# Edge counts from one moving operand, and a new spread of scatters and gathers over the phases

## The reference, cut to what matters

```python
z = jax.ops.segment_sum(ex, dst, num_segments=n)          # attention: sums over the edges of a node
seg = edge_type * n + dst
agg = jax.ops.segment_sum(x[src], seg, num_segments=N_REL * n)
cnt = jax.ops.segment_sum(ones, seg, num_segments=N_REL * n)
mean = agg.reshape(N_REL, n, -1) / jnp.maximum(cnt, 1.0).reshape(N_REL, n, 1)
h1 = jnp.einsum('rni,rio->no', mean, W_rel) + x @ W_root + b_rgcn
deg = jax.ops.segment_sum(ones, dst, num_segments=n) + 1.0
```

## Time and profile before

| | us |
|---|---|
| median of 3 runs (lowest, highest) | 1623.46 (1621.61, 1624.95) |
| the profiled execution's own time | 1636.26 |
| its span | 1634.5 |
| edge, from 0 to | 177.7 |
| g1 to | 237.2 |
| a1 to | 426.8 |
| g2 to | 479.4 |
| a2 to | 542.2 |

### The profile page before, as it was taken

The page is one execution under the profiler, slowest core; times in us unless marked ns, Lnnn a source line. Parts: engine busy times, 40 slices in busy tenths (PEclk is TensorE's granted clock), DMA queues, the critical chain, the costliest instruction groups (busy, mean ns, idle before and its releaser), DMA issues. The chain is left out here.

```text
span 1634.5 us, 30722 instructions
## 1 busy us (share of the span) xinstructions
PE 1325.3 (81%) x9518; PEld 971.8 (59%) x9519; DVE 913.9 (56%) x1669; ACT 650.1 (40%) x954; POOL 607.3 (37%) x737
## 2 busy tenths in 40 slices
PE   8998485781377669987799999999999938749888
PEld 6766464781264446765666666666666626445566
DVE  8941667793254544225556665566666537656710
ACT  8964410881312334004255555455555433022300
POOL 0086555776556100001355555555555510000000
PEclk9999595795587679996899999999999968958989
DMA  1000200000200411008599999899999868233300
GB/s 57 1 1 1 80 16 1 1 1 0 77 10 1 117 58 58 1 19 298 182 260 287 260 277 290 231 291 288 281 279 276 243 177 233 60 119 116 115 20 29
DMA packets 103603, 208.90 MB, mean 128 GB/s; under 512 B 23346, under 2 KB 48399, under 8 KB 103420
## 3 DMA queue, kind: packets, MB, share of 16 engines
q1 hardware_dynamic: 75484, 145.72, 26.1%
q0 software_dynamic: 28064, 62.47, 16.7%
HBM read 195.14 MB, written 36.43 MB: 142 GB/s over the span
## 5 line engine op out<-in xcount | busy, mean ns | idle before, releaser
L641 PE MATMUL r_pO<-ring,r_rowsT 128*128 x2520 | 421.0, 326 | 0.0
L641 PEld LDWEIGHTS r_pO<-ring,r_rowsT 128*128 128x128 f16 x2520 | 243.8, 98 | 153.9
L1695 DVE SCALAR_TENSOR_TENSOR ring<-q_wstage,ring 128x768 f16<-128x768 f32 x198 | 175.2, 953 | 55.6 <-ACT ring L1654 50.2
L1635 POOL DMA_INDIRECT acc_dram<-r_msg,r_scol x70 | 127.9, 1826 | 158.7 <-PE r_pT L1755 98.9
L1654 ACT ACTIVATE ring<-q_wstage 128x768 f16<-128x768 f32 x198 | 148.8, 829 | 26.4 <-issue 26.4
L474 POOL DMA_INDIRECT inv_col<-qinv_dram,pair_col x112 | 119.8, 1070 | 78.9 <-POOL pair_col L487 71.3
L387 PE MATMUL acc<-oh_d,oh_s 125*125 125x512 f16 (+1 forms) x800 | 143.4, 310 | 4.5 <-issue 3.2
L424 POOL DMA_INDIRECT slot_dram<-table_record,table_rowi x80 | 101.7, 1271 | 103.9 <-issue 103.2
L1683 ACT ACTIVATE r_msg<-r_pO,slot_inv 128x768 f32<-128x768 f32 x70 | 62.8, 897 | 192.1 <-PE r_pO L641 159.8
L1702 DVE TENSOR_TENSOR r_rowsT<-r_pT,r_rowsT 128x512 f16<-128x512 f32 x71 | 48.8, 687 | 106.9 <-ACT r_rowsT L1663 97.6
L1755 PE MATMUL r_pT<-r_S,q_parts 128*128 128x128 f16 x852 | 102.0, 223 | 7.6 <-issue 6.8
(11 more groups left out here) (363 smaller groups left out, 2494.1 us busy)
## 6 DMA issues: line engine op xcount, KB each, us to landing
q_wstage<-in_L_gnn_W_rel_dram SPq DMA_DIRECT2D x33, 2304.0 KB
f_stage<-in_L_ffn_w_dram SPq DMA_DIRECT2D x12, 768.0 KB, 4.5
stage<-in_L_gnn_W_dram SPq DMA_DIRECT2D x6, 768.0 KB, 5.7
q_wstage<-in_L_ffn_w_fast_dram SPq DMA_DIRECT2D x6, 768.0 KB, 5.0
q_wstage<-in_L_ffn_w_slow_dram SPq DMA_DIRECT2D x6, 768.0 KB, 7.0
q_wstage<-in_L_ffn_h_fast_dram SPq DMA_DIRECT2D x6, 768.0 KB, 8.7
f_stage<-in_L_ffn_w_fast_dram SPq DMA_DIRECT2D x6, 768.0 KB, 4.4
f_stage<-in_L_ffn_w_slow_dram SPq DMA_DIRECT2D x6, 768.0 KB, 6.0
```

What stands on the lines that cost most here:

```text
L641: ins = eng.matmul(out, x, w[:, h * n:(h + 1) * n], start=first and x is xh and w is wh, stop=last and x is xl, **kw)
L1635: eng.indirect_dma_start(out=K.acc_dram[u % 2], out_offset=bass.IndirectOffsetOnAxis(ap=scol[:, u:u + 1], axis=0), in_=msg[:, u, :], in_of ...
L1695: ins_ = eng.scalar_tensor_tensor(wring[:, slot, 1, k, :], wstage[:, slot, k, :], W_SCALE, wring[:, slot, 0, k, :], ALU.mult, ALU.subtract)
```

## The change

The relation one-hot of a column is no longer a strided view of `R`: VectorE writes it (34 wide) behind the source one-hot in the same place of the ring, which grows to 659 columns. The products are taken the other way round: the destination one-hot is the stationary operand for all, and source and relation are moved through together. A row tile takes two matmuls, of 512 and of 147 columns. The sums stand transposed in PSUM, so that the copies come out as `CT` at once, and `K.counts` is what the transposes give; the mask and the degrees hang on the copies and no longer on the transposes. The scatters run in three blocks, 40 in edge, 28 in g1 and 12 at the start of a1, and the load of the slot table moves behind the last of them, to a1. The gathers are spread as 56 in a1, 20 in g2 and 36 in a2.

```diff
--- before.py
+++ after.py
-TABLED_FIRST = 46
-INV_A1, INV_G2 = 68, 88
+TABLED_EDGES, TABLED_G1 = 40, 68
+INV_A1, INV_G2 = 56, 76
...
-        oh_s = sb("oh_s", [EP, HOTS, N], FP16)
+        oh_s = sb("oh_s", [EP, HOTS, N + REL], FP16)
...
+            TAIL = REST + REL
+
+            def tail_at(i):
+                return 5 + i // 3, i % 3 * TAIL
 
             def count_piece(i, piece):
                 if piece == 0:
                     return acc[0:P, i, :], slice(0, 512)
-                b, o = (5, i * REST) if i < 4 else (6, 0)
-                return acc[0:P, b, o:o + REST], slice(512, N)
+                b, o = tail_at(i)
+                return acc[0:P, b, o:o + TAIL], slice(512, N + REL)
...
-                scatter_records(K, eng, s["tabled"], 0, TABLED_FIRST)
-                eng.wait_ge(s["tabled"], 16 * TABLED_FIRST)
+                scatter_records(K, eng, s["tabled"], 0, TABLED_EDGES)
+                eng.wait_ge(s["tabled"], 16 * TABLED_EDGES)
...
                         eng.wait_ge(s["hots_free"], j + 1)
-                        eng.tensor_scalar(oh_s[:, u, :], iota_n[:, :], srcf[:, j:j + 1], None, ALU.is_equal).then_inc(s["hots_s_ready"], 1)
+                        eng.tensor_scalar(oh_s[:, u, N:], iota_g[0:EP, :], etf[:, j:j + 1], None, ALU.is_equal)
+                        eng.tensor_scalar(oh_s[:, u, 0:N], iota_n[:, :], srcf[:, j:j + 1], None, ALU.is_equal).then_inc(s["hots_s_ready"], 1)
...
                 eng.wait_ge(s["products_done"], 1)
-                a, cols = count_piece(NT - 1, 1)
-                eng.tensor_copy(K.counts[:, NT - 1, cols], a).then_inc(s["rest_stored"], 1)
-                link(eng.tensor_scalar(qinv[:, :, :], acc[0:P, 6, REST:REST + NT * REL].rearrange("p (i r) -> p i r", r=REL), 1.0, W_SCALE,
-                                       ALU.max, ALU.mult))
+                for b, i0, n in ((5, 0, 3), (6, 3, 2)):
+                    tails = acc[0:P, b, 0:n * TAIL].rearrange("p (i r) -> p i r", r=TAIL)
+                    eng.tensor_copy(CT[0:P, i0:i0 + n, 512:N], tails[:, :, 0:REST]).then_inc(s["rest_stored"], 1)
+                    last = eng.tensor_scalar(qinv[:, i0:i0 + n, :], tails[:, :, REST:TAIL], 1.0, W_SCALE, ALU.max, ALU.mult)
+                link(last)
...
                 for i in range(NT):
-                    for piece in range(2 if i < NT - 1 else 1):
-                        a, cols = count_piece(i, piece)
-                        eng.copy(K.counts[:, i, cols], a).then_inc(s["counts_stored"], 1)
+                    eng.copy(CT[:, i, 0:512], acc[0:P, i, :]).then_inc(s["ct_stored"], 1)
...
                     for t in range(NT):
-                        tile = slice(t * P, (t + 1) * P)
-                        at = REST + t * REL
-                        eng.matmul(acc[0:P, 6, at:at + REL], oh_d[:, u, tile], onehot, start=False, stop=False, **kw)
                         for piece in range(2):
                             a, cols = count_piece(t, piece)
-                            last = eng.matmul(a, oh_s[:, u, tile], oh_d[:, u, cols], start=False, stop=False, **kw)
+                            last = eng.matmul(a, oh_d[:, u, t * P:(t + 1) * P], oh_s[:, u, cols], start=False, stop=False, **kw)
...
@@ gat_project, sync @@
-            if heads > 1:
-                eng.wait_ge(s["tabled"], 16 * (EJ - TABLED_FIRST))
-                eng.dma_start(K.table["tables"][:, :, :, :].rearrange("t a l b -> t a (l b)"),
-                              K.slot_dram.rearrange("(a t l) b -> t a (l b)", a=2, l=128)).then_inc(K.s_table_loaded, 16)
@@ gat_project, gpsimd @@
-                scatter_records(K, eng, s["tabled"], TABLED_FIRST, EJ)
+                scatter_records(K, eng, K.s_tabled, TABLED_EDGES, TABLED_G1)
@@ gat_attend, sync @@
+            if heads > 1:
+                eng.wait_ge(K.s_tabled, 16 * (EJ - TABLED_EDGES))
+                eng.dma_start(K.table["tables"][:, :, :, :].rearrange("t a l b -> t a (l b)"),
+                              K.slot_dram.rearrange("(a t l) b -> t a (l b)", a=2, l=128)).then_inc(s["table_loaded"], 16)
@@ gat_attend, gpsimd @@
                 eng.sem_inc(s["out_free"], 2)
+                scatter_records(K, eng, K.s_tabled, TABLED_G1, EJ)
                 eng.wait_ge(s["columns_ready"], 1)
                 gather_inverse_counts(K, eng, s, 0, INV_A1)
```

More of the change, by code:

```diff
@@ L355, in _ @@
                 for i in range(NT):
-                    for piece in range(2 if i < NT - 1 else 1):
-                        a, cols = count_piece(i, piece)
-                        eng.copy(K.counts[:, i, cols], a).then_inc(s["counts_stored"], 1)
+                    eng.copy(CT[:, i, 0:512], acc[0:P, i, :]).then_inc(s["ct_stored"], 1)
                 for i in range(NT):
                     eng.wait_ge(s["transposed"], i + 1)
-                    eng.copy(CT[:, i, :], acc[0:P, 2 * (i % 2):2 + 2 * (i % 2), :].rearrange("p b n -> p (b n)")[:, 0:N]).then_inc(s["ct_stored"], 1)
+                    eng.copy(K.counts[:, i, :], acc[0:P, 2 * (i % 2):2 + 2 * (i % 2), :].rearrange("p b n -> p (b n)")[:, 0:N]).then_inc(s["counts_stored"], 1)
             @block.tensor
@@ L401, in _ @@
                 zeros((6,), P, False, True).then_inc(s["products_done"], 1)
-                eng.wait_ge(s["counts_stored"], 2 * NT - 1)
-                eng.wait_ge(s["rest_stored"], 1)
+                eng.wait_ge(s["ct_stored"], NT)
+                eng.wait_ge(s["rest_stored"], 2)
                 for i in range(NT):
                     if i >= 2:
-                        eng.wait_ge(s["ct_stored"], i - 1)
+                        eng.wait_ge(s["counts_stored"], i - 1)
                     for k in range(NT):
@@ L410, in _ @@
                         lo, hi = k * P, (k + 1) * P
-                        src = K.counts[:, k, i * P:(i + 1) * P]
+                        src = CT[:, k, i * P:(i + 1) * P]
                         if hi <= 512:
@@ L675, in gat_project @@
         W = Weights(K, name + "_w", rows_view(w), B["stage"], B["wparts"])
-        s = {n: K.sem(name + "_" + n) for n in ("a_loaded", "projected", "h_ready", "ones_ready", "pair_ready", "tabled"
+        s = {n: K.sem(name + "_" + n) for n in ("a_loaded", "projected", "h_ready", "ones_ready", "pair_ready"
                                                 ) + tuple("gathered_%d" % b for b in range(IDX_BUFS))}
@@ L764, in gat_attend @@
         s = {n: K.sem(name + "_" + n) for n in ("cs_ready", "als_ready", "max_done", "uv_made", "uv_ready", "bc_ready", "rows_copied", "t1_ready", "arg_ready",
-                                                "e_ready", "p_ready", "pv_done", "out_free", "finish_a", "finish_b", "bias_loaded", "pair_ready", "table_turned", "columns_ready"
+                                                "e_ready", "p_ready", "pv_done", "out_free", "finish_a", "finish_b", "bias_loaded", "pair_ready", "table_loaded", "table_turned", "columns_ready"
                                                 ) + tuple("gathered_%d" % b for b in range(IDX_BUFS))}
@@ L935, in spread_sources @@
                 spread(2 * b, B["cur"][:, b, 0, :]).then_inc(s["als_ready"], 1)
-            turns(eng, spread_sources, between=lambda: turn_tables(K, eng, K.s_table_loaded, psum[:, 6, 0:4 * T1]).then_inc(s["table_turned"], 1))
+            turns(eng, spread_sources, between=lambda: turn_tables(K, eng, s["table_loaded"], psum[:, 6, 0:4 * T1]).then_inc(s["table_turned"], 1))
             def multiply(h, b):
@@ L991, in gat_phase @@
             B["stage"][0:P, :, :].rearrange("p k n -> p (k n)"), B["parts"][:, :, :, :].bitcast(FP32).rearrange("p i a c -> p (i a c)"))]
-        K.s_table_loaded = K.sem("table_loaded")
+        K.s_tabled = K.sem("slots_tabled")
         gat_project(K, "g1", B, B["g"], norm, ins["L0_gnn_W1"], ins["L0_gnn_a_src1"], ins["L0_gnn_a_dst1"], HEADS, HD, h1)
```

5 lines of the change are left out of this document (1 added, 4 removed).

## The result

Twelve runs of each kernel: 1620.54 us median before (1618.25 to 1625.19), 1625.68 after (1623.28 to 1628.76). The ratio after to before is 1.0028, with a 95% interval of 1.0017 to 1.0038: 0.28% or 4.5 us slower (the medians lie 5.1 apart), where 2.4 us faster was forecast. The time lies in the range given, on the other side of no change.

A forecast was written before the change was run, and what follows sets the result against it. TensorE was taken to bound edge and GpSimd a1, with a2 close; edge would become GpSimd's. Edge -10.3, a1 -12.1 and a2 +20.0 made -2.4 us from 1623.46: 1621.1, range 1604 to 1629 (the forecast's own 1615 to 1626).

The forecast's parts named there:

- TensorE's column: Edge phase: a row tile falls from 0.338 to 0.280 us, a column from 1.69 to 1.40.
- rival 3: Edge: TensorE's column does not shrink, phase ends at 159 to 161, total 1629.4 us, slower; chance 0.12.
- The 34-wide one-hots: Edge, VectorE: each added instruction costs 0.09 us, 4 us over 46 columns less 0.9 of waits, ranks 3.2 later.
- The products' end: Edge: VectorE as the late feeder takes TensorE's one-hot products to 132 us.
- The 40 scatters: Edge, GpSimd: first starts at 85.2, all 40 take 64.7 us (bounds 59.4 and 68), ending at 149.9.
- The row shows none of it: Edge: no sign of VectorE's one-hots locking GpSimd's ports; if so, scatters would be held up to 13 us.
- The end of edge: GpSimd takes the bound from TensorE; with landing 1.45 and barrier 0.8 the phase ends at 152.2 us.
- The slow stretch: Edge, 104 to 144 us: TensorE's slowdown, worth 15.2 us, belongs to the profiled execution alone.
- rivals 1 and 2: Edge: slow stretch in every run; 1: goes with the change, 1605.9 us, chance 0.22; 2: stays, 1614.7, chance 0.10.
- a1 and a2: a1: late table +12.2, twelve gathers fewer -24.3, so -12.1 us; a2: twelve more, 24.3 less 4.25 cover, +20.0.
- g1 and g2: 28 scatters in g1 and 20 gathers in g2 bound neither phase: no change.
- the edge term: Edge phase in a plain run: from 162.5 us before to 152.2, a gain of 10.3.

The follow-up runs named there:

- the second profile of before: The unchanged kernel before, profiled once more: span 1620.0 us, g1 starting at 160.67, 359 matmuls from 104 to 144 us; its first profile had span 1634.5.

## Why the prediction was wrong, point by point

**TensorE's column**: right. Forecast 0.280 a tile, 0.284 measured; rival 3 is out. The 0.32 that followed from the Trainium skill (TensorE: Matmul & The Clock Gate, LDWEIGHTS) is not seen either.

**The 34-wide one-hots: the step that failed.** "I take 0.09"; they cost 0.146. The row chosen had an 80-element instruction start 0.11 behind its predecessor, but that is one pair, an arithmetic instruction and a cast, at the start of the kernel. Forecast: ranks 3.2 us later, first scatter at 85.2; measured: 87.61. In the second profile of before it is at 80.87, and the 6.74 us to 87.61 are 46 times 0.146: all 46 stand ahead of the last rank. The 0.9 us of waits that were to vanish were of the first profile.

**The products' end**: forecast 132, measured 135.7. VectorE as the feeder was right, its pace was not.

**The 40 scatters**: forecast 64.7, measured 66.6. "The row shows none of it" was a reading of three one-hots and one scatter. After, one-hots come in longer rows without a pause, and eight scatters of 1.25 to 1.35 us stand beside them, with one-hots of up to 0.70. So the rule of the Trainium skill (SBUF — State Buffer, Who interferes with whom) was waved off too early: the contention is there, at 0.13 for each of the eight, 1.0 us and not 13. Another 0.7 is the scatter beside the 4.1 us operation (4.93 and not 4.26), and 0.2 the first.

**The end of edge**: forecast 152.2, measured 156.7: 2.4 by the ranks, 1.9 by the scatters, 0.2 by the landing. That GpSimd sets it was right.

**The slow stretch**: right that it was of the profiled execution alone, so rivals 1 and 2 are out. But the plain edge phase of before, put at 162.5, was 160.7 in a second profile. So this term, -10.3, was -4.0: 4.5 of the 6.3 on the side of after, 1.8 on that of before.

**a1 and a2**: -12.1 and +20.0 forecast, -12.4 and +20.7 measured. **g1 and g2**: nothing forecast, -0.2 and -0.7.

The sum was -10.3 - 12.1 + 20.0 = -2.4; with the measured terms it is -4.0 - 12.4 + 20.7 = +4.3, and +3.7 with the three small ones. Two large terms that were right to 0.7 left a balance of 8 us against the change, so the sign hung on the edge term. The price of the small one-hots (0.056 us too low, 46 times, 2.6 us) takes the forecast sum to zero by itself; the scatters and the level taken for before, 1.9 and 1.8, turn it. That the time still lies in the range given is owed to the range's width, set for the rivals.

## What to carry to other kernels

Moving a small operation from an engine that bounds a phase to its feeder is priced by the number of the feeder's instructions more than by their elements (0.146 us for 34 here, 0.29 for 625), and one nearest row is not enough where it is taken dozens of times. Before work is moved between phases, ask of each phase who is last in it and by how much: here twelve scatters cost a1 12 us and four would have cost none. When a profile lies 1% above the median, take a second before pricing from it.

## What the runs showed of the hardware

- Beside gathers in a row on GpSimd (1.25 us each) VectorE stood still for 23 to 30 us at a time, and ScalarE and TensorE with it, in some sets of runs and not in others: 1595 or 1664 us for one kernel. The cause is not shown.
- A tensor_tensor of 4.1 us with both operands in SBUF holds an indirect DMA of GpSimd until it ends (4.93 us; 1.46 with the operation cut in eight); beside a tensor_reduce of 4.1 us two took 1.18 and 1.19.
- The stretch in which 40 us held 221 matmuls in one execution and 359 in another, at a granted clock of 1.00 in both, stays unexplained.
